# Two layer norms applied by ScalarE instead of VectorE, their row factors worked out by GpSimd, in a fused attention and feed-forward kernel

## The reference

```python
def layernorm(x):
    return (x - mean(x)) / sqrt(var(x) + 1e-5)          # over the 512 numbers of a row

def attention(x):
    r, k, v = split(x @ W_rkv + b_rkv)
    r, k = sigmoid(r), exp(k);  kv = k * v
    u1, u2 = running sums over time of kv and k, each decayed by lam per step
    return ((u1 + gamma * kv) / (u2 + gamma * k + 1e-6) * r) @ W_o + b_o

def ffn(x):
    prev = x one row earlier (zeros before the first row of a sequence)
    r = sigmoid((mu_r * x + (1 - mu_r) * prev) @ W_r.T)
    k = relu((mu_k * x + (1 - mu_k) * prev) @ W_k.T) ** 2
    return r * (k @ W_v.T)

z = layernorm(x + attention(x))
out = layernorm(z + ffn(z))
```

## Time and profile before

| | |
|---|---|
| time of a run, median of 3 | 2763.93 us (2758.83 to 2767.05) |
| span of the profiled execution | 2760.2 us |
| own device time of the profiled execution beside its span | not given; the median is 3.7 us over the span |
| PE busy | 2582.5 us (94%) |
| DVE busy | 2410.0 us (87%) |
| ACT busy | 1112.7 us (40%) |
| POOL busy | 1227.9 us (44%) |
| mean granted TensorE clock | 0.980 of full |

### The profile page before, as it was taken

How to read it: one execution, slowest core, us unless ns; L and a number is a source line. 1 busy time by engine, 2 the same in 40 slices (tenths; PEclk the granted TensorE clock), 3 DMA queues, 4 the chain that set the end, 5 groups by cost and what they waited for, 6 DMA issues and landing times.

```text
span 2760.2 us, 36072 instructions
## 1 busy us (share of the span) xinstructions
PE 2582.5 (94%) x12800; PEld 2185.4 (79%) x12800; DVE 2410.0 (87%) x3275; ACT 1112.7 (40%) x1935; POOL 1227.9 (44%) x779
## 2 busy tenths in 40 slices
PE   7899999999999999999999999999999999999997
PEld 5678887778887788877888877887788877788886
DVE  8898898888898888998889989889888899898884
ACT  4334343434443343443434443434434343434343
POOL 3444444444443444544444434445344444444453
PEclk9999999999999999999999999999999999999998
DMA  4011011011011110100111101101001111011000
GB/s 164 8 39 47 31 47 35 27 48 47 31 42 36 33 47 31 47 31 32 47 35 42 39 24 46 46 31 47 31 31 46 31 48 39 24 46 47 31 31 24
DMA packets 57806, 110.94 MB, mean 40 GB/s; under 512 B 7040, under 2 KB 7040, under 8 KB 57088
## 3 DMA queue, kind: packets, MB, share of 16 engines
q1 hardware_dynamic: 57600, 108.31, 11.8%
HBM read 74.73 MB, written 33.55 MB: 39 GB/s over the span
## 4 chain that ended last, share of the span: by engine, by line
PE 48%; DVE 24%; issue 16%; POOL 8%; ACT 2%; DMA 1%; SPq 0%; DVEq 0%; POOLq 0%; ACTq 0%
PE bankB L792 7%; PE bankB L790 7%; PE bankB L791 7%; PE bankA L773 5%; PE bankA L774 5%; PE bankA L775 5%; PE bankB L838 5%; PE bankB L840 4%; PE bankB L839 4%; DVE xk_f L662 3%; DVE att_f L616 3%; POOL rstd L317 3%; POOL att_f L308 3%; DVE key L601 3%; DVE xr_f L662 3%
## 5 line engine op out<-in xcount | busy, mean ns | idle before, releaser
L773 PE MATMUL bankA<-x_hi,wrkv_hi 128*128 128x512 f32 x1536 | 611.0, 398 | 81.5 <-DVE kv L595 58.4
L774 PE MATMUL bankA<-x_lo,wrkv_hi 128*128 128x512 f32 x1536 | 603.4, 393 | 0.0
L775 PE MATMUL bankA<-x_hi,wrkv_lo 128*128 128x512 f32 x1536 | 602.6, 392 | 0.0
L308 POOL TENSOR_TENSOR att_f<-att_f,gate 128x512 f32<-128x512 f32 x128 | 204.7, 1599 | 594.3 <-DVE att_f L621 594.3
L608 DVE RECIPROCAL gate<-gate 128x512 f32<-128x512 f32 x128 | 429.2, 3353 | 4.4
L773 PEld LDWEIGHTS bankA<-x_hi,wrkv_hi 128*128 128x128 f32 x1536 | 291.4, 190 | 154.9 <-DVE kv L595 71.9
L838 PE MATMUL bankB<-xk_hi,wk_hi 128*128 128x256 f32 x1024 | 305.7, 298 | 69.4 <-ACT zT L438 67.4
L775 PEld LDWEIGHTS bankA<-x_hi,wrkv_lo 128*128 128x128 f32 x1536 | 291.2, 190 | 62.2
L774 PEld LDWEIGHTS bankA<-x_lo,wrkv_hi 128*128 128x128 f32 x1536 | 291.7, 190 | 56.4
L417 ACT ACTIVATE key<-bankA,b_sb 128x512 f32<-128x512 f32 x128 | 86.6, 676 | 562.6 <-PE bankA L775 550.3
L330 POOL TENSOR_TENSOR t<-t,y 128x512 f32<-128x512 f32 x128 | 191.5, 1517 | 257.2 <-DVE t L682 257.2
(11 more groups left out here) (84 smaller groups left out, 6020.0 us busy)
## 6 DMA issues: line engine op xcount, KB each, us to landing
x_f<-in_xT SPq DMA_DIRECT2D x128, 256.0 KB, 3.9
y<-in_x SPq DMA_DIRECT2D x128, 256.0 KB, 2.7
out<-t SPq DMA_DIRECT2D x128, 256.0 KB, 2.0
wrkv_f<-in_w_rkv SPq DMA_DIRECT2D x3, 768.0 KB, 6.8
wo_f<-in_w_o SPq DMA_DIRECT2D x1, 1024.0 KB, 10.2
wr_f<-in_w_r SPq DMA_DIRECT2D x1, 1024.0 KB, 12.0
wk_f<-in_w_k SPq DMA_DIRECT2D x1, 1024.0 KB, 13.9
wv_f<-in_w_v SPq DMA_DIRECT2D x1, 1024.0 KB, 15.8
```

Source lines behind the costliest of these rows:

```text
L308: pool.tensor_tensor(att_f[:, c], att_f[:, c], gate[:, c % 2], ALU.mult).then_inc(att_made, 1)
L773: pe.matmul(bank[:], w_hi, x_hi[:, h], start=(h == 0), stop=False)
L774: pe.matmul(bank[:], w_hi, x_lo[:, h], start=False, stop=False)
L775: last = pe.matmul(bank[:], w_lo, x_hi[:, h], start=False, stop=(h == NC - 1))
```

## The change

`normalise` moves from VectorE to ScalarE: an activation Identity with a per-row scale (`rstd`) and a per-row bias (`shift` = -mean times `rstd`) in place of the subtraction and multiplication. `inverse_std` on GpSimd grows from one small instruction to four. The small instruction on `zT` goes to ScalarE, at the end of `mixed_high`. VectorE loses L637, L653, L666 and L668. Four constants are made by GpSimd at the start. In `last_block` VectorE's order is also changed (both `attention_rows` come first), and GpSimd's.

```diff
         @block.gpsimd
+            pool.memset(zT[:, :, 0:1], 0.0).then_inc(s_col0, 1)
+            pool.memset(zero[:], 0.0).then_inc(s_const, 1)
+            pool.memset(half_pow[:], -0.5).then_inc(s_const, 1)
+            pool.memset(eps_ln[:], EPS_LN).then_inc(s_const, 1)
...
             def inverse_std(s, which, half):
+                tiles = slice(HT * half, HT * half + HT)
+                wait(pool, ln_mean[which], s.count(NT, HT * half + HT))
+                pool.tensor_tensor(ve[:, which, tiles], mv[:, which, tiles, 1], eps_ln[:], ALU.add)\
+                    .then_inc(ln_var[which], 1)
+                pool.tensor_tensor(shift[:, which, tiles], zero[:, 0:HT, 0], mv[:, which, tiles, 0], ALU.subtract)\
+                    .then_inc(ln_negated[which], 1)
                 wait(pool, ln_var[which], s.count(NH, half + 1))
-                tiles = slice(HT * half, HT * half + HT)
                 pool.tensor_tensor(rstd[:, which, tiles], ve[:, which, tiles], half_pow[:], ALU.pow)\
                     .then_inc(ln_rstd[which], 1)
+                wait(pool, ln_negated[which], s.count(NH, half + 1))
+                wait(pool, ln_rstd[which], s.count(NH, half + 1))
+                pool.tensor_tensor(shift[:, which, tiles], shift[:, which, tiles], rstd[:, which, tiles], ALU.mult)\
+                    .then_inc(ln_shift[which], 1)
...
         @block.scalar
+            def normalise(s, which, half, rows, done):
+                wait(act, ln_shift[which], s.count(NH, half + 1))
+                for i in range(HT):
+                    tile = HT * half + i
+                    act.activation(rows(tile), rows(tile), ACT.Identity, bias=shift[:, which, tile:tile + 1],
+                                   scale=rstd[:, which, tile:tile + 1]).then_inc(done, 1)
...
             def mixed_high(s, half, run):
...
+                if half == NH - 1 and s.back(-1).first_of_batch():
+                    act.activation(zT[:, :, 0:1], zero[:], ACT.Copy).then_inc(s_col0, 1)
+                else:
+                    act.activation(zT[:, :, 0:1], zT[:, :, HALF:HALF + 1], ACT.Copy).then_inc(s_col0, 1)
...
             (scalar) def step(s):
                 exp_gate(s, 0)
+                if s1.exists():
+                    normalise(s1, 0, 0, z_rows(s1), z_made)
                 exp_key(s, 1)
+                if s.back(2).exists():
+                    normalise(s.back(2), 1, 1, result_rows(s.back(2)), out_made)
                 if s1.exists():
                     copy_zT(s1, 0)
+                    normalise(s1, 0, 1, z_rows(s1), z_made)
                     previous_scaled(s1, 0, s)
                 att_high(s, 0)
                 exp_gate(s, 1)
...
                 att_high(s, 3)
                 if s1.exists():
+                    normalise(s1, 1, 0, result_rows(s1), out_made)
                     tanh(s1, 1)
                     key_square(s1, 1)
...
         @block.vector
-                wait(dve, ln_mean[which], s.count(NT, HT * half + HT))
-                tiles = slice(HT * half, HT * half + HT)
-                dve.tensor_scalar(ve[:, which, tiles], mv[:, which, tiles, 1], EPS_LN, None, ALU.add)\
-                    .then_inc(ln_var[which], 1)
...
-            def normalise(s, which, half, rows, done):
-                wait(dve, ln_rstd[which], s.count(NH, half + 1))
-                for i in range(HT):
-                    tile = HT * half + i
-                    dve.tensor_scalar(rows(tile), rows(tile), mv[:, which, tile, 0:1], rstd[:, which, tile:tile + 1],
-                                      ALU.subtract, ALU.mult).then_inc(done, 1)
...
-                if next_starts_batch:
-                    dve.memset(zT[:, :, 0:1], 0.0).then_inc(s_col0, 1)
-                else:
-                    dve.tensor_copy(zT[:, :, 0:1], zT[:, :, HALF:HALF + 1]).then_inc(s_col0, 1)
```

More of the change, by code:

```diff
@@ L143, in program @@
         half_pow = sb("half_pow", [P, HT])
+        eps_ln = sb("eps_ln", [P, HT])
+        held = sb("held", [P, 1])
         st = sb("st", [P, 2, NT, 6])
-        held = sb("held", [P, 1])
         mv = sb("mv", [P, 2, NT, 2])
@@ L148, in program @@
         rstd = sb("rstd", [P, 2, NT])
+        shift = sb("shift", [P, 2, NT])
+        zero = sb("zero", [P, NC, 1])
         bankA = [ctx.enter_context(nc.psum_tensor(f"bankA{i}", [P, TB], F32)) for i in range(NBANK)]
@@ L193, in program @@
         ln_rstd = [sem(f"ln{i}_rstd") for i in (1, 2)]
+        ln_negated = [sem(f"ln{i}_negated") for i in (1, 2)]
+        ln_shift = [sem(f"ln{i}_shift") for i in (1, 2)]
         zT_copied, xk_scaled, xr_scaled = sem("zT_copied"), sem("xk_scaled"), sem("xr_scaled")
@@ L377, in last_block @@
                 residual(s2, 1)
+                inverse_std(s1, 0, 1)
                 inverse_std(s2, 1, 1)
                 mixed_low(s1, 0, s)
-                inverse_std(s1, 0, 1)
                 mixed_low(s1, 1, s)
@@ L447, in previous_scaled, with result_rows, z_rows @@
                             .then_inc(made, 1)
+            def normalise(s, which, half, rows, done):
[4 more added lines that the diff above has]
+                                   scale=rstd[:, which, tile:tile + 1]).then_inc(done, 1)
+            def result_rows(s):
+                return lambda tile: t[:, tile]
+            def z_rows(s):
+                return lambda tile: y[:, y_slot(s, tile)]
             def mixed_high(s, half, run):
@@ L535, in last_block @@
             def last_block(s):
-                s1 = s.back(1)
+                s1, s2 = s.back(1), s.back(2)
+                normalise(s1, 0, 0, z_rows(s1), z_made)
                 copy_zT(s1, 0)
                 previous_scaled(s1, 0, s)
+                normalise(s1, 0, 1, z_rows(s1), z_made)
+                normalise(s2, 1, 1, result_rows(s2), out_made)
                 mixed_high(s1, 0, s)
@@ L546, in last_block @@
                 tanh(s1, 1)
+                normalise(s1, 1, 0, result_rows(s1), out_made)
             def last_half(s):
-                pass
+                normalise(s.back(2), 1, 1, result_rows(s.back(2)), out_made)
             steps(act, step, last_block, last_half)
@@ L647, in attention_rows, with mix @@
                 statistics(s, 0, half, lambda tile: y[:, y_slot(s, tile)], y_made)
-            def normalise(s, which, half, rows, done):
-                wait(dve, ln_rstd[which], s.count(NH, half + 1))
-                for i in range(HT):
-                    tile = HT * half + i
-                    dve.tensor_scalar(rows(tile), rows(tile), mv[:, which, tile, 0:1], rstd[:, which, tile:tile + 1],
-                                      ALU.subtract, ALU.mult).then_inc(done, 1)
-            def mix(s, half, next_starts_batch, run):
+            def mix(s, half, run):
                 for f, which, scaled, made in r_and_k(run, (xr_f, 0, xr_scaled, xr_made),
@@ L686, in result_rows @@
                 return lambda tile: t[:, tile]
-            def z_rows(s):
-                return lambda tile: y[:, y_slot(s, tile)]
             def step(s):
@@ L701, in step @@
                 if s1.exists():
-                    normalise(s1, 0, 0, z_rows(s1), z_made)
                     attention_rows(s1, 1)
[L704 to L707, removed]
                 numerator(s, 0)
                 if s1.exists():
-                    mix(s1, 0, False, s)
+                    mix(s1, 0, s)
                 denominator(s, 1)
@@ L716, in step @@
                     key_low(s1, 0)
-                    mix(s1, 1, s.first_of_batch(), s)
+                    mix(s1, 1, s)
                 if first:
@@ L727, in step @@
                     statistics(s1, 1, 0, result_rows(s1), y2_made)
-                    normalise(s1, 1, 0, result_rows(s1), out_made)
                     key_low(s1, 1)
@@ L734, in last_block @@
                 gated_values(s2, 1)
-                normalise(s1, 0, 0, z_rows(s1), z_made)
+                attention_rows(s1, 1)
                 statistics(s2, 1, 1, result_rows(s2), y2_made)
[L737 to L740, removed]
+                mix(s1, 0, s)
                 key_low(s1, 0)
-                mix(s1, 1, True, s)
+                mix(s1, 1, s)
                 gated_values(s1, 0)
                 statistics(s1, 1, 0, result_rows(s1), y2_made)
-                normalise(s1, 1, 0, result_rows(s1), out_made)
                 key_low(s1, 1)
@@ L751, in last_half @@
                 statistics(s2, 1, 1, result_rows(s2), y2_made)
-                normalise(s2, 1, 1, result_rows(s2), out_made)
             steps(dve, step, last_block, last_half)
```

2 lines of the change are left out of this document (removed).

## The result

| | before | after |
|---|---|---|
| time, median | 2762.02 us (2758.83 to 2767.05, 4 runs) | 2700.31 us (2696.96 to 2705.98, 4 runs) |
| span of the profiled execution | 2760.2 us | 2697.3 us (its own device time 2699.09) |
| DVE, ACT, POOL busy | 87%, 40%, 44% | 76%, 48%, 48% |
| mean granted TensorE clock | 0.980 | 0.987 |

The ratio is 0.977, with a 95% interval of 0.9752 to 0.9789: faster by 2.3%. The prediction was 2696, with a range of 2632 to 2745.

What follows compares the result with a forecast made beforehand. TensorE was taken to lose 155 us in 30 periods, mostly waiting for VectorE's `kv` and `zT`. With 91 left, 64 gained plus about 4 in the opening gave a span of 2692 and a median of 2696 us, range 2632 to 2745.

Steps and rivals of the forecast that it cites:

- The stop before P22 goes: TensorE's wait for `kv` before P22 vanishes with 1.7 us to spare, worth 1.5 to 1.6 us a step.
- The stop before K0 shrinks from 2.2 + 1.5 to 1.6: Before K0: L605 falls into `xr_lo`, numerator at E + 11.4; a stop of 1.6 us stays of 3.7, 48 in all.
- A new stop before V2: At the step's turn V2 waits 1.0 us for `ka_lo`, behind ScalarE's norm on `t`: 24 us in 24 steps.
- The low clock: TensorE at half speed stays behind a third of the stops that have it now: 6 x 1.5 = 9 us.
- The opening: At the start, the long P22 stop and the 0.85 us behind it give back about 4 us.
- The drain: At the end, one short stop less and 1 us more at the last norm: nothing in all.
- The engines' busy times: Over the whole run, VectorE busy about 2120 us and ScalarE about 1310 us.
- The rival in which both products are caught: Before K0: L601 caught by `xr_lo`, L605 by `xk_lo`; stop of 4.5 us, time 2800 us; chance 0.08.
- The rival in which L605 escapes: Before K0: L605 escapes `xr_lo`, K0's stop goes, V2's stays; time 2638 us; chance 0.24.

Runs made afterwards that it cites:

- e6: The changed kernel with the column of `zT` copied on VectorE again, at the end of `mix`: 2700.64 us, ratio 0.9777.
- e3: The changed kernel with `xr_lo` and `xk_lo` on GpSimd each done as four instructions instead of one: 2679.64 us, ratio 0.9692.
- e9: e8 with `xr_lo` and `xk_lo` also ahead of `att_lo` of group 0 on GpSimd: 2760.47 us, ratio 0.9974.
- e8: The changed kernel with the high parts of xr and xk on ScalarE ahead of `att_high(0)` and the gate of group 1: 2696.34 us, ratio 0.976.
- e1: The changed kernel with the second norm of half 0 (on `t`) moved behind `tanh` and `key_square` on ScalarE: 2691.58 us, ratio 0.9751.
- e2: The changed kernel with the second norm of half 1 moved on ScalarE from ahead of `copy_zT` to behind the gate of group 1: 2639.44 us, ratio 0.9551.
- e4: The changed kernel with both moves of e1 and e2 together: 2607.51 us, ratio 0.9437.
- e5: The kernel before the change with only the column of `zT` moved to ScalarE, the norms left as they were: 2759.03 us, ratio 0.9981.

## Why the prediction was right

Step by step:

- **The stop before P22 goes.** Right. The scan of group 1 starts 0.44 behind the last scaled row (0.42 was worked out), and P22 never waits in a steady step. In e6, with the copy back on VectorE, it does not wait either, so it is the norms' move that took the stop away.
- **The stop before K0 shrinks from 2.2 + 1.5 to 1.6.** Right in mechanism, short in size: 1.8 to 2.0, together 58 where 48 was forecast. From the end E = 673.46 of the scaled rows, L648 ends at E + 6.1 (forecast 6.0), the numerator at E + 11.5 (11.4), K0 starts 3.5 later. The whole chain of catches (`att_lo` beside the scan, L601 behind `att_lo`, L605 behind `xr_lo`) is in the rows. That the end of L605 fits to 0.1 is in part luck: `xr_lo` took 2.77 and not 2.4, and the product needed 0.54 behind it and not 0.7. What is off is TensorE's side: it wants K0 20.8 us behind the start of the key of group 1 on ScalarE, where the old trace less its idle times gives 21.1. A stop costs more than its idle time. In the old trace P22 started 1.88 behind the matmul before it where 0.23 is the undisturbed distance, which is 1.65 for 1.50 idle, and its twelve matmuls took 2.88 where twelve take 2.73. The prediction took off only the idle time, so its 704.62 is 0.3 too late and its stop 0.3 too short, 9 us in 30 steps. e3 and e9 show that the catches are on the path: a shorter one brings K0's stop from 1.96 to 0.91, a second one brings it from 1.83 (e8) to 3.06.
- **A new stop before V2.** Right: 0.8 in 23 steps (1.0 in 24 was forecast), 19 us for 24. GpSimd's four small instructions take 1.34 from start to end (1.5). e1 takes the stop away. ScalarE's pair takes 1.43 from start to start (1.45) and one norm 0.81 (0.78), though no row ahead of the prediction shows the share of the row operand from which these were worked out.
- **The low clock.** 6 stretches that cost 1.5 each were forecast, and 6 are seen in the steady steps; a period with one lasts 80.7 without its stops, the others 79.2. The cost was read rightly, the number was luck: it came from a guess that a third would stay, and in e1 as many stops before K0, of the same length, had 20.
- **The opening** gave 6 instead of 4. **The drain** cost 3.9 instead of nothing, a mis-sized term. TensorE's stops there are 13.2 where they were 10.3: the last block's K0 now waits 3.88 for `xk_lo`, whose high part stands behind two pairs of norms on ScalarE, and a V2 waits 2.06 for `key_square`, while the waits for the first norm fell from 8.4 to 5.3.
- **The engines' busy times.** ScalarE 1288 (1310 forecast), VectorE 2045 (2120): the sixteen additions of `mix` in a step, L694, take 74 us less than before (480 ns each for 604 and 645), which the forecast left as they were.

The sum: 48 + 24 + 10 + 9 = 91 us of loss in the 30 periods were forecast, and 94.3 measured. They are 58.2 + 19.3 + 9.9 in stops and 9 at the low clock, less 2 because the undisturbed rest of a period lasts 79.19 and not 79.26. With 6.0 gained and 3.9 lost outside them the span fell by 62.9 instead of 68.

The rival in which both products are caught did not come, but the double catch exists: e9 has it. Its stop is 3.1, not the 4.5 worked out, and the time 2760, not 2800. The two are not the same case: in e9 `xr_lo` starts 1.4 ahead of the product L644 (L601 before), at E + 1.0, while the rival let both become free at about the same moment, so that the product waits for nearly all of it. What that would cost stays untested.

The rival in which L605 escapes (2638) has the time of e2, 2639.44, but not its account: it left out that the scan behind the reciprocal can be caught by `xk_lo`, and 1.2 of e2's 1.8 us came from the shorter queue. In e8, where only the product comes free, the stop stays at 1.8.

The rule of the Trainium skill ("SBUF — State Buffer", "Who interferes with whom"), that the order of issue decides and that the second waits for the end of the first, is borne out: L648 starts ahead of `xr_lo` in e2 and takes 0.69, behind it in the changed kernel and takes 2.77. What is left of its own time then is measured: a product ends 0.54 behind the GpSimd instruction. The rule against elementwise work on ScalarE ("ScalarE: Activation LUTs" of the Trainium skill, "Rules for kernel authors") holds for one instruction here, 0.81 against 0.55, and would have misled as a verdict on the whole.

Open: why the low clock follows some stops before K0 and not others of the same length (6 against 20 stretches). Its cost is most of the reason why e1 gains less than it frees, and why e4 gains more than the sum of e1 and e2.

## What to carry to other kernels

What an engine's removed work is worth is read from the chain ahead of the stop that it feeds, and an instruction that waits for a shared port must be followed to its successor: the wait passed to that one in e2, e5 and e8. When work moves between engines, write out for the next few instructions who meets whom; here the order of the same instructions decided between 2607 and 2760 us (e4, e9). And look behind the moved work on its new engine: a norm that nobody needs soon belongs behind the chain that TensorE waits for (e1, e2), not ahead of it.

## What was not expected of the hardware

- A VectorE scan that meets a GpSimd instruction ends 1.1 us behind it, almost its full 1.2 later (e5), while products of two tensors end 0.54 behind (679.56 against 679.02), less than their 0.69.
- Cutting a 128x1024 subtraction on GpSimd into four costs: 3.4 us instead of 2.6 (e3).
- A stop of TensorE costs more than the idle time that is shown for it: about 0.3 us more at P22 (1.88 + 2.88 us from start to start, where 0.23 + 2.73 are undisturbed, with 1.50 idle).
- Taking away one kind of stop brought the low clock behind another kind (e1): mean granted clock 0.974 to 0.979 in four runs, 0.984 to 0.988 in those of the changed kernel, 0.977 to 0.980 in seven of the kernel before.
